# The first 40 microseconds of a fused graph kernel: second batch's xT loaded ahead of adj, its product with W0 made directly behind the first batch's, and the first loads issued from two queues in fewer requests

## The chip, the cores and the metric

The kernel runs on one core of one Trainium2 chip. The metric is the device time of one execution in microseconds. Before the change the median of three runs is 545.93 us (545.26 to 547.8).

## What is computed

There are 16 batches. Each has x (512 nodes by 256 features) and its own adjacency matrix adj (512 by 512). Two blocks follow each other, each with a residual and a layer norm:

```python
# block 0 (layer norm 1 behind it)
h = x @ W0 + b0
x = layernorm(x + (adj @ h) / adj.sum(-1))
# block 1 (layer norm 2 behind it)
y = relu(adj @ (x @ W1) + b1)
y = relu(adj @ (y @ W2) + b2)
x = layernorm(x + adj @ (y @ W3) + b3)
```

All is fp32. The kernel makes each fp32 product from three products of rounded parts: every operand is split into a "hi" part (rounded) and a "lo" part (what is left), and hi·hi, lo·hi and hi·lo are added up in PSUM.

## The kernel before

Nodes lie on the 128 partitions in T = 4 tiles, features in KF = 2 halves. A batch goes through eight products on TensorE (PE), named by their helper functions: `p0` (xT times W0, into h), `p1` (adj times h), `p2` (x1 times adj, into g), `p3` (W1 times g, into x2), `p4` (x2 times W2, into s2), `p5`, `p6` and `p7` (the third layer). `three_passes` issues the three matmuls of one product; they show as lines 180, 181 and 182. Behind each product ScalarE (ACT) rounds the result into a hi tile (`copy_hi`, line 486) and VectorE (DVE) subtracts it into a lo tile (`sub_hi`, line 676). GpSimd (POOL) makes the lo tiles of adj, adds b0 and b3, and in the first microseconds makes some lo tiles of x1 and the weights.

`norm1` is the first layer norm. On DVE it takes one tile a turn: a reciprocal of the row sum (it waits for `p1_done` of that tile), a scalar_tensor_tensor into v1 (it waits for POOL's `xb`, x plus b0), bn_stats and bn_aggr, and in the next turn, when ACT has made the square root (`std_1`), x1. A turn's x1 is what `p2` needs.

Every engine works through its own instructions in the order of the code, and waits on semaphores. In the steady part a loop runs `step(new)` for batch after batch, in which the products of two or three batches are interleaved by hand. Ahead of the loop stands a prologue, written out by hand for each engine, that brings batches `FIRST` and `second` to where the loop takes over; the loop's first matmul is that of `p5(FIRST)`. SP (the sync engine) issues all loads, in one queue. The second batch's xT goes into the buffer `y`, its x into `v` (`v2`), its adjT into `adj_rows`, since those aren't needed yet.

In the prologue `p1_first`, `p2_first` and `p0_first` are forms of the products that start as soon as the first operands are there. PE's prologue before:

```python
p0_first()
p1_first(range(0, T // 2)); p1_first(range(T // 2, T))
p0(second, None, None, bank_a)
p2_first(range(0, 1)); p1(second, range(0, 1))
p2_first(range(1, T)); p1(second, range(1, 2))
p3(FIRST); p1(second, range(2, 3))
p4(FIRST); p1(second, range(3, T))
```

and DVE's, of which the second half (from `norm1(FIRST, range(3, ...))` on) is the same in both kernels but for a split of W1:

```python
split_xT(second, 0); split_xT(second, 1)
norm1(FIRST, range(0, 3)); h(second, bank_a)
norm1(FIRST, range(3, T + 2)); norm1(second, range(0, 1))
g(FIRST, 0); g(FIRST, 1); norm1(second, range(1, 2))
x2(FIRST, 0); x2(FIRST, 1); norm1(second, range(2, 3))
s2(FIRST); norm1(second, range(3, T + 2))
```

Of the kernel before, what the change touches and what calls it, by code (L numbers as in the profile page):

```python
# [18 lines left out]

def build(nc, xT, x, adjT, adj, w0, w1, w2, w3, b0, b1, b2, b3, out):  # L20
    NB = x.shape[0]
# [7 lines left out]
    with ExitStack() as ctx:  # L29
# [12 lines left out]
        b0_all = sb("b0_all", [P, F], F32)
        b3_all = sb("b3_all", [P, F], F32)
        b1_col = sb("b1_col", [P, KF], F32)
        b2_col = sb("b2_col", [P, KF], F32)
# [53 lines left out]
        adj0_even_split = sem("adj0_even_split")  # L99
        x1_first_split = sem("x1_first_split")  # L100
# [106 lines left out]
        def _(sp):  # L207
# [17 lines left out]
            for half in range(2):  # L225
                tiles = half_of(half, T)
                sp.dma_start(adj1_raw[:, tiles, :], adjT[1, :, tiles, :]).then_inc(adj1_loaded[half], DMA)
            sp.dma_start(w_raw[:, 1, :, :], w1).then_inc(w_loaded[1], DMA)
            sp.dma_start(x1_raw[:, :, :], x[1]).then_inc(x1_loaded, DMA)
            sp.dma_start(b3_all[:, :], b3.partition_broadcast(P)).then_inc(b_loaded[3], DMA)  # L230
            sp.dma_start(w_raw[:, 2, :, :], w2).then_inc(w_loaded[2], DMA)
            sp.dma_start(b1_col[:, :], b1).then_inc(b_loaded[1], DMA)
            sp.dma_start(b2_col[:, :], b2).then_inc(b_loaded[2], DMA)
            sp.dma_start(w_raw[:, 3, :, :], w3).then_inc(w_loaded[3], DMA)

# [248 lines left out]
        def _(act):  # L484
# [115 lines left out]
            def step(new, last=False, ahead=True):  # L600
# [21 lines left out]
            split_adj(FIRST, 0)  # L622
            h(FIRST, tiles=range(0, 1))
            split_adj(FIRST, 1)
            h(FIRST, tiles=range(1, 3))
            split_adj(FIRST, 2)
            h(FIRST, tiles=range(3, T))
            split_adj(FIRST, 3)
# [8 lines left out]
            h(second, bank_a, range(0, 1))
            x1_split_hi(FIRST, 0)
            h(second, bank_a, range(1, T))
            std_1(FIRST, 2)  # L640
            x1_split_hi(FIRST, 1)
            split_w(1)
            std_1(FIRST, 3)
            x1_split_hi(FIRST, 2)
            x1_split_hi(FIRST, 3)
            norm1(second, None, range(0, 1))
# [215 lines left out]
        def _(pool):  # L862
# [55 lines left out]

            for k in range(0, T, 2):
                pool.wait_ge(adj_hi_ready, k + 1)  # L920
                pool.tensor_tensor(adj_lo[:, 0, k, :], adj_raw[:, k, :], adj_hi[:, 0, k, :].bitcast(F32),
                                   ALU.subtract).then_inc(adj0_even_split, 1)
            pool.wait_ge(b_loaded[0], DMA)
# [11 lines left out]
            pool.wait_ge(b_loaded[3], DMA)  # L935
            add_b3(FIRST, range(0, 2))
# [45 lines left out]
```

## Time and profile before

| | |
|---|---|
| median of three runs | 545.93 us |
| the profiled execution: its own time, its span | 545.0 us, 543.2 us |
| PE busy | 531.9 us, 98% of the span |
| DVE, ACT, POOL busy | 351.8, 311.0, 212.1 us |
| all idle time of PE that the waits list | 6.6 us, all of it in the first 38 us |
| granted TensorE clock, mean | 0.994 |
| DMA | 58.23 MB, mean 107 GB/s |

The span is what the profiler saw from the first to the last instruction. PE's busy share is near one from slice to slice; only the first two slices of 40 and the last one are lower. The prologue ends at 41.56 us, when the loop's first matmul starts.

### The profile page before, as it was taken

What the parts mean: (1) busy time and instruction counts of PE and PEld (TensorE: products, weight loads), DVE (VectorE), ACT (ScalarE), POOL (GpSimd) and SP (SyncE); (2) the same over time, 40 slices, a digit from 0 to 9 for tenths busy, and PEclk for the clock granted to TensorE, in tenths of its full rate; (3) what the DMA queues carried; (4) which work ended last, traced back from release to release, by engine and by line L of the source; (5) the groups of instructions that cost most, each with busy time, mean ns of one, the idle gap of its engine ahead of it and who ended that gap; (6) DMA issues with size and microseconds to landing.
All of it is one profiled execution on the core that took longest, in us unless ns stands there. A gap on an engine that the chain in (4) does not pass through costs nothing.

```text
span 543.2 us, 10642 instructions
## 1 busy us (share of the span) xinstructions
PE 531.9 (98%) x3637; PEld 490.4 (90%) x3637; DVE 351.8 (65%) x1058; ACT 311.0 (57%) x786; POOL 212.1 (39%) x228
## 2 busy tenths in 40 slices
PE   7899999999999999999999999999999999999996
PEld 6878999989899898999989899898998989899896
DVE  4774675757667485675757667475675757657546
ACT  4555655566555746655566554756655566564542
POOL 2866318072360904408062270814509063271100
PEclk9999999999999999999999999999999999999998
DMA  8630060602507043070612507033070511600002
GB/s 275 226 140 1 30 244 0 238 36 65 206 0 270 0 137 133 11 259 0 214 56 60 211 0 270 0 124 146 0 270 0 192 79 50 222 1 40 1 1 78
DMA packets 15286, 58.23 MB, mean 107 GB/s; under 512 B 1952, under 2 KB 2720, under 8 KB 13472
## 3 DMA queue, kind: packets, MB, share of 16 engines
q1 hardware_dynamic: 15264, 57.94, 29.5%
q8 instruction: 13, 0.21, 0.2%
q14 instruction: 9, 0.07, 0.0%
HBM read 49.55 MB, written 8.39 MB: 107 GB/s over the span
## 4 chain that ended last, share of the span: by engine, by line
PE 92%; DVE 4%; DMA 2%; ACT 1%; issue 1%; SPq 1%; DVEq 0%
PE bank_a L181 16%; PE bank_a L182 16%; PE bank_a L180 16%; PE bank_b L180 14%; PE bank_b L182 14%; PE bank_b L181 14%; DMA y<-in_xT 2%; PE bank_b L273 1%; PE bank_b L274 1%; DVE x L744 0%; DVE v L737 0%; DVE xT_lo L676 0%; DVE stats L748 0%; DVE x_lo L676 0%; DVE stats L787 0%
## 5 line engine op out<-in xcount | busy, mean ns | idle before, releaser
L900 POOL TENSOR_TENSOR adj_lo<-adj_raw,adj_hi 128x512 fp32r<-128x512 f32 x56 | 70.8, 1298 | 264.2 <-ACT adj_hi L486 264.2
L676 DVE TENSOR_TENSOR x_lo<-bank_a,x_hi 128x512 fp32r<-128x512 f32 x62 | 42.8, 691 | 67.7 <-ACT bank_a L576 67.7
L180 PE MATMUL bank_b<-h_hi,adj_hi 128*128 128x256 f32 (+1 forms) x256 | 71.7, 280 | 2.2 <-DVE h_lo L676 2.2
L551 ACT ACTIVATE std<-moments,eps_col 128x1 f32<-128x1 f32 x64 | 18.9, 295 | 92.4 <-DVE moments L757 92.4
L182 PE MATMUL bank_b<-h_hi,adj_lo 128*128 128x256 f32 (+1 forms) x256 | 71.5, 279 | 0.0
L181 PE MATMUL bank_b<-h_lo,adj_hi 128*128 128x256 f32 (+1 forms) x256 | 71.5, 279 | 0.0
L182 PE MATMUL bank_b<-s_hi,adj_lo 128*128 128x256 f32 x232 | 64.1, 276 | 0.0
L180 PE MATMUL bank_b<-s_hi,adj_hi 128*128 128x256 f32 x232 | 64.0, 276 | 0.0
L181 PE MATMUL bank_b<-s_lo,adj_hi 128*128 128x256 f32 x232 | 64.0, 276 | 0.0
L574 ACT ACTIVATE x_hi<-bank_a,b_col 128x512 fp32r<-128x512 f32 x62 | 42.4, 684 | 21.4 <-PE bank_a L182 20.2
L882 POOL TENSOR_TENSOR x1b<-x,b_all 128x256 f32<-128x256 f32 x64 | 46.0, 754 | 17.2 <-DVE x L744 17.2
L180 PEld LDWEIGHTS bank_b<-h_hi,adj_hi 128*128 128x128 f32 x256 | 48.9, 191 | 2.3 <-issue 2.3
L180 PE MATMUL bank_a<-adj_hi,s_hi 128*128 128x512 f32 x128 | 50.1, 391 | 0.0
L181 PE MATMUL bank_a<-adj_lo,s_hi 128*128 128x512 f32 x128 | 50.0, 390 | 0.0
L182 PE MATMUL bank_a<-adj_hi,s_lo 128*128 128x512 f32 x128 | 49.8, 389 | 0.0
L181 PEld LDWEIGHTS bank_b<-h_lo,adj_hi 128*128 128x128 f32 x256 | 48.8, 191 | 0.0
L182 PEld LDWEIGHTS bank_b<-h_hi,adj_lo 128*128 128x128 f32 x256 | 48.8, 191 | 0.0
L595 ACT ACTIVATE std<-moments,eps_col 128x1 f32<-128x1 f32 x64 | 18.9, 295 | 51.9 <-DVE moments L799 51.9
L676 DVE TENSOR_TENSOR g_lo<-bank_a,g_hi 128x512 fp32r<-128x512 f32 x30 | 20.7, 691 | 40.2 <-ACT g_hi L486 40.2
L180 PE MATMUL bank_a<-adj_hi,x_hi 128*128 128x512 f32 x120 | 46.7, 389 | 0.0
L181 PE MATMUL bank_a<-adj_lo,x_hi 128*128 128x512 f32 x120 | 46.7, 389 | 0.0
L182 PE MATMUL bank_a<-adj_hi,x_lo 128*128 128x512 f32 x120 | 46.7, 389 | 0.0
(145 smaller groups left out, 1653.8 us busy)
## 6 DMA issues: line engine op xcount, KB each, us to landing
adj_raw<-in_adjT SPq DMA_DIRECT2D x30, 512.0 KB, 5.4
adj_rows<-in_adj SPq DMA_DIRECT2D x14, 1024.0 KB, 9.4
x_raw<-in_x SPq DMA_DIRECT2D x15, 512.0 KB, 7.4
out_y<-y SPq DMA_DIRECT2D x15, 512.0 KB, 2.9
xT_raw<-in_xT SPq DMA_DIRECT2D x14, 512.0 KB, 6.5
w_raw<-in_w SPq DMA_DIRECT2D x4, 256.0 KB, 10.2
adj_rows<-in_adjT SPq DMA_DIRECT2D x2, 512.0 KB, 10.1
xT_raw<-in_xT SPq DMA_DIRECT2D x2, 256.0 KB, 3.6
```

The source lines that it names most:

```text
L180: pe.matmul(acc, st[0], mv[0], start=start, stop=False)
L181: pe.matmul(acc, st[0], mv[1], start=False, stop=False)
L182: return pe.matmul(acc, st[1], mv[0], start=False, stop=stop)
L273: pe.matmul(bank[j][:, 0:2 * F], hi, w_both[:, n, k, :, :], start=True, stop=False)
L274: mm = pe.matmul(bank[j][:, 0:F], lo, mv[0], start=False, stop=False)
L551: act.activation(std1[:, j:j + 1], moments1[:, j, 1:2], ACT.Sqrt, bias=eps_col[:, :]).then_inc(std1_ready, 1)
L574: act.activation(hi[:, f, :], bank[:, :], ACT.Relu, bias=bias[:, f:f + 1])
L595: act.activation(std2[:, j:j + 1], moments2[:, j, 1:2], ACT.Sqrt, bias=eps_col[:, :]).then_inc(std2_ready, 1)
L676: return dve.tensor_tensor(lo, full, hi.bitcast(F32), ALU.subtract)
L882: pool.tensor_tensor(x1b[:, slot(batch), j, :], x1[:, j, :], b3_all[:, :], ALU.add).then_inc(x1b_ready, 1)
L900: pool.tensor_tensor(adj_lo[:, s, k, :], raw[:, k, :], adj_hi[:, s, k, :].bitcast(F32), ALU.subtract).then_inc(adj_split, 1)
```

## The change

It has four parts, all in the prologue; the loop and the end are untouched.

1. Loads. SP issues xT of batch 0 in one request, adjT's low half, b0 with b3 in one, the second adjT's low half, x of the second batch, W1 to W3 in one, b1 with b2 in one. ACT issues W0 and the second batch's xT at its very start, and behind its table load adjT's high half, x of batch 0 and the second adjT's high half. The host lays W1 to W3, b0 with b3, and b1 with b2 side by side for this.
2. PE. `p0(second)` stands directly behind `p0_first`. `p1_first` goes tile by tile. `p2_first` is made in one piece; `p1(second)` tile 0 stands behind it, tiles 1 and 2 behind `p3`, tile 3 behind `p4`.
3. ACT and DVE split the second batch's xT ahead of the first batch's h tiles 1 to 3 and of adj. POOL makes the lo part of one adj tile of batch 0 and DVE of three (before two and two). DVE makes W1's lo part.
4. ACT's order behind that: a `std_1`, an `x1_split_hi` and a `split_adj(second)` alternate; `h(second)` comes behind `std_1(FIRST, 2)` and waits for all of `p1_first`.

```diff
@@ sync @@
-            sp.dma_start(w_raw[:, 0, :, :], w0).then_inc(w_loaded[0], DMA)
-            for half in range(2):
-                tiles = half_of(half, T)
-                sp.dma_start(xT_raw[:, tiles, :], xT[0, :, tiles, :]).then_inc(xT0_loaded[half], DMA)
...
-            sp.dma_start(x_raw[:, :, :], x[0]).then_inc(x_loaded, DMA)
-            sp.dma_start(b0_all[:, :], b0.partition_broadcast(P)).then_inc(b_loaded[0], DMA)
-            sp.dma_start(xT1_raw[:, :, :], xT[1]).then_inc(xT_loaded, DMA)
...
+            sp.dma_start(xT_raw[:, :, :], xT[0]).then_inc(xT_loaded, DMA)
+            low = half_of(0, T)
+            sp.dma_start(adj_raw[:, low, :], adjT[0, :, low, :]).then_inc(adj_loaded[0], DMA)
+            sp.dma_start(b03_all[:, :], b03.partition_broadcast(P)).then_inc(b03_loaded, DMA)
+            sp.dma_start(adj1_raw[:, low, :], adjT[1, :, low, :]).then_inc(adj1_loaded[0], DMA)
+            sp.dma_start(x1_raw[:, :, :], x[1]).then_inc(x1_loaded, DMA)
+            sp.dma_start(w_raw[:, 1:4, :, :], w123).then_inc(w123_loaded, DMA)
+            sp.dma_start(b12_col[:, 0:2 * KF], b12).then_inc(b12_loaded, DMA)
@@ tensor @@
             p0_first()
+            p0(second, None, None, bank_a)
             pe.wait_ge(ones_set, 2 * T)
-            p1_first(range(0, T // 2))
-            p1_first(range(T // 2, T))
-
-            p0(second, None, None, bank_a)
-            p2_first(range(0, 1))
+            for j in range(T):
+                p1_first(range(j, j + 1))
+            p2_first(range(0, T))
             p1(second, range(0, 1))
-            p2_first(range(1, T))
-            p1(second, range(1, 2))
-            pe.wait_ge(w_split, 1)
+            pe.wait_ge(w1_split, 1)
             p3(FIRST)
-            p1(second, range(2, 3))
-            pe.wait_ge(w_split, 3)
+            p1(second, range(1, 3))
+            pe.wait_ge(w_split, 2)
             p4(FIRST)
             p1(second, range(3, T))
@@ scalar @@
+            high = slice(T // 2, T)
+            act.dma_start(w_raw[:, 0, :, :], w0).then_inc(w0_loaded, DMA)
+            act.dma_start(xT1_raw[:, :, :], xT[1]).then_inc(xT1_loaded, DMA)
             act.wait_ge(eps_set, 1)
             act.activation(sqrt_eps[:, :], eps_col[:, :], ACT.Sqrt)
+            act.dma_start(adj_raw[:, high, :], adjT[0, :, high, :]).then_inc(adj_loaded[1], DMA)
+            act.dma_start(x_raw[:, :, :], x[0]).then_inc(x_loaded, DMA)
+            act.dma_start(adj1_raw[:, high, :], adjT[1, :, high, :]).then_inc(adj1_loaded[1], DMA)
...
+            act.wait_ge(p1_done, T)
+            h(second, bank_a)
+            x1_split_hi(FIRST, 2)
             split_adj(second, 3)
...
@@ vector @@
-            h(FIRST, tiles=range(0, 2))
-            split_adj0(1)
-            h(FIRST, tiles=range(2, T))
-            split_adj0(3)
+            h(FIRST, tiles=range(0, 1))
             split_xT(second, 0)
             split_xT(second, 1)
+            h(FIRST, tiles=range(1, T))
+            split_adj0(0)
+            split_adj0(2, counts=2)
+            split_adj0(3)
             norm1(FIRST, range(0, 3))
             h(second, bank_a)
             norm1(FIRST, range(3, T + 2))
+            split_w1()
             norm1(second, range(0, 1))
             g(FIRST, 0)
             g(FIRST, 1)
@@ gpsimd @@
-            split_adj(second, range(0, 3))
+            split_adj(second, range(0, 1))
             split_x1_first(0)
+            split_adj(second, range(1, 2))
+            split_x1_first(1)
+            split_adj(second, range(2, 3))
+            split_x1_first(2)
             split_adj(second, range(3, T))
-            split_x1_first(1)
             add_b0(second, range(0, 1))
-            split_x1_first(2)
-            split_w(1)
             add_b0(second, range(1, T))
```

The order of PE's products from `p2_first` to the loop, one row for each product, before (`bank_b` with `x1_hi` is `p2_first`, `bank_a` with `h_hi` is `p1(second)` and its number is the tile, `bank_b2<-g_hi` begins `p3`, `bank_b0<-w_both,x2_hi` begins `p4`):

```order
L180 MATMUL bank_b0<-adj_hi,x1_hi 128x512
...
L180 MATMUL bank_a0<-h_hi,adj_hi 128x258
...
L180 MATMUL bank_b0<-adj_hi,x1_hi 128x512
...
L180 MATMUL bank_a1<-h_hi,adj_hi 128x258
...
L180 MATMUL bank_b2<-g_hi,w_both 128x512
...
L180 MATMUL bank_a2<-h_hi,adj_hi 128x258
...
L180 MATMUL bank_b0<-w_both,x2_hi 128x256
...
L180 MATMUL bank_a3<-h_hi,adj_hi 128x258
```

The same stretch of PE in the changed kernel:

```order
L184 MATMUL bank_b0<-adj_hi,x1_hi 128x512
...
L184 MATMUL bank_a0<-h_hi,adj_hi 128x258
...
L184 MATMUL bank_b2<-g_hi,w_both 128x512
...
L184 MATMUL bank_a1<-h_hi,adj_hi 128x258
...
L184 MATMUL bank_a2<-h_hi,adj_hi 128x258
...
L184 MATMUL bank_b0<-w_both,x2_hi 128x256
...
L184 MATMUL bank_a3<-h_hi,adj_hi 128x258
```

Tile 0 of `p1(second)` moved from inside `p2_first` to behind it, and tile 1 from ahead of `p3` to behind it. DVE's instructions between them did not move: this is DVE in the changed kernel, from the reciprocal of the second batch's tile 0 (`inv_rows<-bank_a`) to the lo parts of g and the reciprocal of tile 1:

```order
L726 RECIPROCAL inv_rows<-bank_a 128x1
L736 SCALAR_TENSOR_TENSOR v<-bank_a,inv_rows,xb 128x256
L747 BN_STATS stats<-v 128x6
L756 BN_AGGR moments<-stats 128x2
L670 TENSOR_TENSOR g_lo<-bank_b,g_hi 128x512 x2
L726 RECIPROCAL inv_rows<-bank_a 128x1
```

So tile 0 of norm1(second) still stands ahead of g's lo parts on DVE, and tile 1 ahead of x2's. ACT around `h(second)` before, from the split of the last xT half to its fourth h tile (`h_hi<-bank_a` are the h tiles of the second batch):

```order
L486 ACTIVATE xT_hi<-y 128x512 x2
L486 ACTIVATE adj_hi<-adj_rows 128x512
L551 ACTIVATE std<-moments,eps_col 128x1
L486 ACTIVATE adj_hi<-adj_rows 128x512 x2
L551 ACTIVATE std<-moments,eps_col 128x1
L486 ACTIVATE adj_hi<-adj_rows 128x512
L486 ACTIVATE h_hi<-bank_a 128x256
L486 ACTIVATE x_hi<-x 128x256
L486 ACTIVATE h_hi<-bank_a 128x256 x3
```

And ACT in the changed kernel, from the first h tile of batch 0 to the same place:

```order
L474 ACTIVATE h_hi<-bank_b 128x256
L474 ACTIVATE xT_hi<-y 128x512 x2
L474 ACTIVATE h_hi<-bank_b 128x256 x3
L474 ACTIVATE adj_hi<-adj_raw 128x512 x4
L474 ACTIVATE adj_hi<-adj_rows 128x512
L542 ACTIVATE std<-moments,eps_col 128x1
...
L474 ACTIVATE adj_hi<-adj_rows 128x512
L542 ACTIVATE std<-moments,eps_col 128x1
L474 ACTIVATE h_hi<-bank_a 128x256 x4
```

The second batch's xT now comes ahead of all four adj tiles of the first, and the h tiles of the second batch come behind the third `std` instead of the second.

## Rows read from the trace of the kernel before

**Rows 1.** Windows: length, busy (instructions) of PE, PEld, DVE, ACT, POOL, PEclk, DMA share, GB/s

```profile
9.00:11.40 2.40, 0.42 (x3) 0.45 (x4) 1.37 (x4) 2.40 (x8) 1.38 (x2) 0.99 0.94 352
11.40:14.70 3.30, 3.30 (x18) 3.30 (x17) 2.44 (x5) 1.80 (x5) 3.30 (x4) 0.50 1.02 414
41.60:75.00 33.40, 33.40 (x231) 30.80 (x231) 21.02 (x64) 18.67 (x48) 13.22 (x14) 1.00 0.23 82
```

**Rows 2.** The chain that ended last, 0 to 45 us: start, length, what

```profile
1.80 0.42 SPq L217
...
2.74 0.43 SPq L221
3.21 0.43 SPq L222
...
4.16 9.18 DMA y<-in_xT
...
14.03 2.15 DVE xT_lo L676 x2
...
22.02 1.30 DVE h_lo L676 x4
...
30.75 1.30 DVE g_lo L676 x2
```

**Rows 3.** DMA issues of single loads: out, in, KB, us from issue to landing

```profile
xT_raw<-in_xT SPq DMA_DIRECT2D x1, 256.0 KB, 3.7
...
adj_raw<-in_adjT SPq DMA_DIRECT2D x1, 512.0 KB, 7.2
x_raw<-in_x SPq DMA_DIRECT2D x1, 512.0 KB, 8.0
```

**Rows 4.** Timeline of PE: start, length, line, what, and the idle time ahead

```profile
5.63 0.47 PE L309 MATMUL bank_b<-w_both,xT_hi 128*128 128x256 f32 x2 [0.58 <-ACT xT_hi L486]
...
8.43 0.39 PE L315 MATMUL bank_b<-w_both,xT_lo 128*128 128x256 f32 x2
10.98 0.36 PE L180 MATMUL bank_b<-h_hi,adj_hi 128*128 128x258 f32 x1 [2.16 <-DVE h_lo L676]
...
29.82 0.39 PE L182 MATMUL bank_b<-adj_hi,x_lo 128*128 128x512 f32 x1
...
32.19 0.47 PE L180 MATMUL bank_b<-g_hi,w_both 128*128 128x512 f32 x1 [0.54 <-DVE g_lo L676]
...
35.02 0.28 PE L180 MATMUL bank_a<-h_hi,adj_hi 128*128 128x258 f32 x1
...
36.32 0.28 PE L182 MATMUL bank_a<-h_hi,adj_lo 128*128 128x258 f32 x1
37.32 0.36 PE L180 MATMUL bank_b<-w_both,x_hi 128*128 128x256 f32 x1 [0.73 <-DVE x_lo L676]
...
41.56 0.40 PE L180 MATMUL bank_a<-adj_hi,s_hi 128*128 128x512 f32 x1
```

**Rows 5.** Timeline of DVE

```profile
12.11 1.06 DVE L676 TENSOR_TENSOR adj_lo<-adj_raw,adj_hi 128x512 fp32r<-128x512 f32 x1
...
16.10 0.15 DVE L727 RECIPROCAL inv_rows<-bank_b 128x1 f32<-128x1 f32 x1
...
28.42 0.15 DVE L727 RECIPROCAL inv_rows<-bank_a 128x1 f32<-128x1 f32 x1
...
29.73 0.18 DVE L757 BATCH_NORM_AGGREGATE moments<-stats 128x2 f32<-128x6 f32 x1
...
31.96 0.16 DVE L727 RECIPROCAL inv_rows<-bank_a 128x1 f32<-128x1 f32 x1
...
33.72 0.18 DVE L757 BATCH_NORM_AGGREGATE moments<-stats 128x2 f32<-128x6 f32 x1
```

**Rows 6.** Timeline of ACT and of POOL

```profile
19.70 0.62 ACT L486 ACTIVATE adj_hi<-adj_rows 128x512 fp32r<-128x512 f32 x1
...
12.58 4.20 POOL L876 TENSOR_TENSOR xb<-x_raw,b_all 128x256 f32<-128x256 f32 x4
```

More of the change, by code:

```diff
@@ L17, with build @@
 WARM = 18
-def build(nc, xT, x, adjT, adj, w0, w1, w2, w3, b0, b1, b2, b3, out):
+def build(nc, xT, x, adjT, adj, w0, w123, b03, b12, out):
     NB = x.shape[0]
@@ L41, in build @@
         w_raw = sb("w_raw", [P, 4, KF, F], F32)
[L42 to L45, printed above, removed]
+        b03_all = sb("b03_all", [P, 2 * F], F32)
+        b0_all, b3_all = b03_all[:, 0:F], b03_all[:, F:2 * F]
+        b12_col = sb("b12_col", [P, 16], F32)
+        b1_col, b2_col = b12_col[:, 0:KF], b12_col[:, KF:2 * KF]
         zeros = sb("zeros", [P, F], F32R)
@@ L89, in build @@
         bank_a = [ctx.enter_context(nc.psum_tensor(f"bank_a{j}", [P, 512], F32)) for j in range(T)]
-        w_loaded = [sem(f"w{n}_loaded") for n in range(4)]
-        b_loaded = [sem(f"b{n}_loaded") for n in range(4)]
-        xT0_loaded = [sem(f"xT0_half{n}_loaded") for n in range(2)]
+        w0_loaded = sem("w0_loaded")
+        w123_loaded = sem("w123_loaded")
+        b03_loaded = sem("b03_loaded")
+        b12_loaded = sem("b12_loaded")
+        xT1_loaded = sem("xT1_loaded")
         xT_loaded = sem("xT_loaded")
@@ L98, in build @@
         adj1_loaded = [sem(f"adj1_half{n}_loaded") for n in range(2)]
-        adj0_even_split = sem("adj0_even_split")
+        adj0_second_split = sem("adj0_second_split")
         x1_first_split = sem("x1_first_split")
@@ L109, in build @@
         w_hi_ready = sem("w_hi_ready")
+        w1_split = sem("w1_split")
         w_split = sem("w_split")
@@ L213, in _ @@
             sp.sem_inc(rows_ready, 2 * T)
-            sp.dma_start(w_raw[:, 0, :, :], w0).then_inc(w_loaded[0], DMA)
-            for half in range(2):
-                tiles = half_of(half, T)
-                sp.dma_start(xT_raw[:, tiles, :], xT[0, :, tiles, :]).then_inc(xT0_loaded[half], DMA)
-            for half in range(2):
-                tiles = half_of(half, T)
-                sp.dma_start(adj_raw[:, tiles, :], adjT[0, :, tiles, :]).then_inc(adj_loaded[half], DMA)
-            sp.dma_start(x_raw[:, :, :], x[0]).then_inc(x_loaded, DMA)
-            sp.dma_start(b0_all[:, :], b0.partition_broadcast(P)).then_inc(b_loaded[0], DMA)
-            sp.dma_start(xT1_raw[:, :, :], xT[1]).then_inc(xT_loaded, DMA)
[L225 to L228, printed above, removed]
-            sp.dma_start(x1_raw[:, :, :], x[1]).then_inc(x1_loaded, DMA)
[L230 to L234, printed above, removed]
+            sp.dma_start(xT_raw[:, :, :], xT[0]).then_inc(xT_loaded, DMA)
[3 more added lines that the diff above has]
+            sp.dma_start(adj1_raw[:, low, :], adjT[1, :, low, :]).then_inc(adj1_loaded[0], DMA)
+            sp.dma_start(x1_raw[:, :, :], x[1]).then_inc(x1_loaded, DMA)
+            sp.dma_start(w_raw[:, 1:4, :, :], w123).then_inc(w123_loaded, DMA)
+            sp.dma_start(b12_col[:, 0:2 * KF], b12).then_inc(b12_loaded, DMA)
             def load(i):
@@ L322, in p1_first @@
                     pe.wait_ge(h_split, max(k + 1, len(tiles)))
-                    if k % 2 == 0:
-                        pe.wait_ge(adj0_even_split, k // 2 + 1)
+                    if k == 1:
+                        pe.wait_ge(adj0_second_split, 1)
                     else:
@@ L488, in split_w @@
             def split_w(n):
-                act.wait_ge(w_loaded[n], DMA)
+                act.wait_ge(w123_loaded, DMA)
                 copy_hi(w_hi[:, n, :, :], w_raw[:, n, :, :]).then_inc(w_hi_ready, 1)
@@ L495, in split_xT @@
                 tiles = slice(half * T // 2, (half + 1) * T // 2)
-                if nxt is FIRST:
-                    act.wait_ge(xT0_loaded[half], DMA)
+                if nxt is second:
+                    act.wait_ge(xT1_loaded, DMA)
+                elif nxt is FIRST:
+                    act.wait_ge(xT_loaded, DMA)
                 else:
                     act.wait_ge(xT_loaded, at(nxt, DMA, 0))
+                if nxt is not FIRST:
                     act.wait_ge(p0_done, at(nxt, T, 0))
@@ L616, in step @@
                     norm1(nxt, before(new, -2) if ahead else None)
+            high = slice(T // 2, T)
+            act.dma_start(w_raw[:, 0, :, :], w0).then_inc(w0_loaded, DMA)
+            act.dma_start(xT1_raw[:, :, :], xT[1]).then_inc(xT1_loaded, DMA)
             act.wait_ge(eps_set, 1)
             act.activation(sqrt_eps[:, :], eps_col[:, :], ACT.Sqrt)
+            act.dma_start(adj_raw[:, high, :], adjT[0, :, high, :]).then_inc(adj_loaded[1], DMA)
+            act.dma_start(x_raw[:, :, :], x[0]).then_inc(x_loaded, DMA)
+            act.dma_start(adj1_raw[:, high, :], adjT[1, :, high, :]).then_inc(adj1_loaded[1], DMA)
             split_xT(FIRST, 0)
             split_xT(FIRST, 1)
-            split_adj(FIRST, 0)
             h(FIRST, tiles=range(0, 1))
[L624 to L628, printed above, removed]
             split_xT(second, 0)
             split_xT(second, 1)
+            h(FIRST, tiles=range(1, T))
+            for k in range(T):
+                split_adj(FIRST, k)
             split_adj(second, 0)
             std_1(FIRST, 0)
+            x1_split_hi(FIRST, 0)
             split_adj(second, 1)
+            std_1(FIRST, 1)
+            x1_split_hi(FIRST, 1)
             split_adj(second, 2)
-            std_1(FIRST, 1)
+            std_1(FIRST, 2)
+            act.wait_ge(p1_done, T)
+            h(second, bank_a)
+            x1_split_hi(FIRST, 2)
             split_adj(second, 3)
[L637 to L641, printed above, removed]
+            std_1(FIRST, 3)
+            x1_split_hi(FIRST, 3)
             split_w(1)
[L643 to L646, printed above, removed]
             g(FIRST, 0)
             g(FIRST, 1)
+            norm1(second, None, range(0, 1))
             split_w(2)
             split_w(3)
-            act.wait_ge(b_loaded[1], DMA)
-            act.wait_ge(b_loaded[2], DMA)
+            act.wait_ge(b12_loaded, DMA)
             x2(FIRST, 0)
@@ L682, in split_xT, with split_adj0, split_w1 @@
                 sub_hi(xT_lo[:, tiles, :], raw[:, tiles, :], xT_hi[:, tiles, :]).then_inc(xT_split, 1)
-            def split_adj0(k):
+            def split_adj0(k, counts=1):
                 dve.wait_ge(adj_hi_ready, k + 1)
-                sub_hi(adj_lo[:, 0, k, :], adj_raw[:, k, :], adj_hi[:, 0, k, :]).then_inc(adj_split, 2)
+                sub_hi(adj_lo[:, 0, k, :], adj_raw[:, k, :], adj_hi[:, 0, k, :]).then_inc(adj_split, counts)
+            def split_w1():
+                dve.wait_ge(w_hi_ready, 1)
+                sub_hi(w_lo[:, 1, :, :], w_raw[:, 1, :, :], w_hi[:, 1, :, :]).then_inc(w1_split, 1)
             def join(bank, half):
@@ L821, in _ @@
                 dve.memset(h_lo[:, j, F:F + ONES].bitcast(F32), 0.0).then_inc(ones_set, 1)
-            dve.wait_ge(w_loaded[0], DMA)
+            dve.wait_ge(w0_loaded, DMA)
             dve.tensor_copy(w_hi[:, 0, :, :], w_raw[:, 0, :, :]).then_inc(w0_hi_ready, 1)
@@ L828, in _ @@
             split_xT(FIRST, 1)
-            h(FIRST, tiles=range(0, 2))
-            split_adj0(1)
-            h(FIRST, tiles=range(2, T))
-            split_adj0(3)
+            h(FIRST, tiles=range(0, 1))
             split_xT(second, 0)
             split_xT(second, 1)
+            h(FIRST, tiles=range(1, T))
+            split_adj0(0)
+            split_adj0(2, counts=2)
+            split_adj0(3)
             norm1(FIRST, range(0, 3))
@@ L917, in step @@
                 add_b3(new)
[L919 to L923, printed above, removed]
+            pool.wait_ge(adj_hi_ready, 2)
+            pool.tensor_tensor(adj_lo[:, 0, 1, :], adj_raw[:, 1, :], adj_hi[:, 0, 1, :].bitcast(F32),
+                               ALU.subtract).then_inc(adj0_second_split, 1)
+            pool.wait_ge(b03_loaded, DMA)
             add_b0(FIRST)
             pool.wait_ge(adj_split, T)
-            split_adj(second, range(0, 3))
+            split_adj(second, range(0, 1))
             split_x1_first(0)
+            split_adj(second, range(1, 2))
+            split_x1_first(1)
+            split_adj(second, range(2, 3))
+            split_x1_first(2)
             split_adj(second, range(3, T))
-            split_x1_first(1)
             add_b0(second, range(0, 1))
-            split_x1_first(2)
-            split_w(1)
             add_b0(second, range(1, T))
-            pool.wait_ge(b_loaded[3], DMA)
             add_b3(FIRST, range(0, 2))
@@ L966 @@
     }
-    for n, name in enumerate(("L0_gnn_W", "L1_gnn_W1", "L1_gnn_W2", "L1_gnn_W3")):
-        arrays[f"w{n}"] = np.asarray(inputs[name]).reshape(KF, P, F).transpose(1, 0, 2)
-    arrays["b0"] = np.asarray(inputs["L0_gnn_b"])
-    arrays["b1"] = np.asarray(inputs["L1_gnn_b1"]).reshape(KF, P).T
-    arrays["b2"] = np.asarray(inputs["L1_gnn_b2"]).reshape(KF, P).T
-    arrays["b3"] = np.asarray(inputs["L1_gnn_b3"])
+    w = [np.asarray(inputs[name]).reshape(KF, P, F).transpose(1, 0, 2)
+         for name in ("L0_gnn_W", "L1_gnn_W1", "L1_gnn_W2", "L1_gnn_W3")]
+    arrays["w0"] = w[0]
+    arrays["w123"] = np.stack(w[1:], axis=1)
+    arrays["b03"] = np.concatenate([np.asarray(inputs["L0_gnn_b"]), np.asarray(inputs["L1_gnn_b3"])])
+    arrays["b12"] = np.concatenate([np.asarray(inputs["L1_gnn_b1"]).reshape(KF, P).T,
+                                    np.asarray(inputs["L1_gnn_b2"]).reshape(KF, P).T], axis=1)
     arrays = {f"in_{k}": np.ascontiguousarray(a) for k, a in arrays.items()}
```

## The prediction

> **What bounds the kernel now.** I read the windows first. In the loop PE is busy for all of 33.40 us in a stretch of 33.40, at the full granted clock [rows 1]. So nothing that only shortens another engine's work counts there, and since the loop's code is untouched, the change is worth what it moves the loop's first matmul, which starts at 41.56 [rows 4]. The rest of the program then follows at the same distance.
>
> Next, the chain that ended last, for the first 45 us. It does not start at adj but at the second batch's xT: its load is issued at 4.16 and takes 9.18 us, so it lands at 13.34; the two xT_lo on DVE keep that engine until 16.1; then comes norm1 of the first batch [rows 2, 5]. The timeline of PE shows what is lost meanwhile: PE idles 2.16 us ahead of `p1_first` (10.98) [rows 4], and from 11.40 to 14.70 the granted clock is 0.50, the lower of its two levels (1.2 GHz) [rows 1]. Eighteen matmuls took 3.30 us there, which at full clock would take half, so that stretch costs 1.65 us. These two, together 3.8 us, are what the change can reach for, and `p0(second)` placed in the gap is the way to it.
>
> I cut the prologue at five places, all read off the rows. S is the start of norm1(FIRST) on DVE, 16.10 [rows 5]. The last h_lo of the second batch ends at 22.02 + 1.30 = 23.32 [rows 2], 7.22 later. The last matmul of `p2_first` starts at 29.82, 6.50 later; `p3` at 32.19, 2.37 later; `p4` at 37.32, 5.13 later; the loop at 41.56, 4.24 later [rows 4]. Together 16.10 + 7.22 + 6.50 + 2.37 + 5.13 + 4.24 = 41.56.
>
> **Term 1, the start of norm1(FIRST).** Before, 768 KB (W0 and the first xT) were down at 1.80 + 3.7 = 5.5, 1792 KB (with adjT) at 2.74 + 7.2 = 9.9, and 2304 KB at 3.21 + 8.0 = 11.2 [rows 2, 3]. From 9 to 14.7 the 16 DMA engines were busy for 0.94 to 1.02 of the time, at 352 to 414 GB/s [rows 1]: they were full from one queue. I therefore take that a second queue brings no more bytes and that the two share in turns. Then W0 and xT land together at about 5.5, and the second xT and adjT's low half together after 1792 KB, at 9.9. `p0_first` took 5.63 to 8.82 [rows 4]; it now starts some 0.5 us later, because the first xT half no longer lands ahead and DVE gets W0 later, and it ends at 9.3 to 9.9. ACT can't overwrite xT_hi before that. So whether the second xT lands at 5.5 (alone and first) or at 9.9 hardly matters; only if it came with 2304 KB, at 11.2, would it cost another 1.3 us. From landing to the first xT_lo took 0.69 us (13.34 to 14.03) [rows 2], and the lo itself takes 0.7 to 1.1 (half of 2.15, with POOL working beside it). PE idles until about 11.4, then makes `p0(second)`: 24 matmuls, which with twelve of `p1` take 4.24 us ahead of the loop, where twelve of `p1` alone take 35.02 to 36.44, 1.42; so 2.82, until 14.2 [rows 4]. Behind xT_hi ACT has three h and four adj copies, at up to 0.62 each [rows 6]; the third lo tile of adj that DVE makes (0.7 to 1.06 each [rows 5]) comes at 15.3 to 15.9, and the first tile of `p1_first` is done 0.6 later, at about 16.3.
>
> The other leg is x: it needs 3584 KB ahead of it and with it, which is 1.84 MB more than at 9.9, or 4.4 to 5.2 us at the rates above, so it lands at 14.3 to 15.1; the first xb on POOL follows in 1.05 (a quarter of 4.20) [rows 6]. That gives 15.4 to 16.2. So S is about 16.3, not earlier than the 16.10 of before: what the early xT gives DVE, the late adj and PE's new order take. Bounds: 15.0 if both queues together run ahead of the old byte count, 17.8 if the gap of PE (9.9 to 11.4) is again followed by a stretch at 0.50 as in rows 1, which would add 1.65. The 2.16 gap did that; this one is some 1.5, and I leave it out.
>
> The Trainium skill, DMA: Bandwidth & Descriptors, section "Issuing engines are not separate DMA queues", says that DMAs of all issuing engines run on the same 16 DMA engines and that a second issuer saves only sequencer time. By that the landings stay as just worked out; if two queues did carry twice the bytes, x would be down before 12 and S would be PE's leg alone, near 15.
>
> **Term 2, to the end of h_lo.** In the order of ACT the h tiles of the second batch now stand behind the third std and a split of adj. DVE's turns of norm1 are as before, so ACT's copies come on top: between none and two at 0.62 [rows 6]. I take 0.9: 8.1 instead of 7.22.
>
> **Term 3, to the last matmul of p2_first.** The chain is norm1's last tile, and stays: 6.5. PE has less to do inside it, since `p1(second)` tile 0 is no longer between the pieces, but that doesn't move the chain's end.
>
> **Term 4, to p3.** Here a wait is added. DVE's order has norm1(second) tile 0 ahead of g's two lo tiles, and it waits for `p1(second)` tile 0, which before was long done and now runs behind `p2_first`. From the last `p2_first` matmul: 0.23 for it; 1.58 for the twelve matmuls and their drain (35.02 to 36.60) [rows 4]; norm1 of one first tile, 28.42 to 29.91, 1.49 [rows 5]; two g_lo and PE's start, 30.75 to 32.19, 1.44 [rows 2, 4]. Sum 4.74 instead of 2.37. PE idles some 3.1 us of it.
>
> **Term 5, to p4.** The same again one step on: norm1(second) tile 1 stands ahead of x2's lo tiles on DVE and waits for `p1(second)` tile 1, which now runs behind `p3`. `p3` 2.83 (32.19 to 35.02), tile 1 of `p1` 1.58 [rows 4], norm1 of a later tile 31.96 to 33.90, 1.94 [rows 5], of which I take 1.7 since POOL has gone quiet by then; two lo tiles and PE's start 1.44 as above. Sum 7.55 instead of 5.13. Term 6, `p4` and tile 3, stays 4.24: tile 2 is already made.
>
> **Term 7, the clock.** The idle 3.1 us ahead of `p3` is longer than the 2.16 us that went before the half clock of rows 1. I count one such stretch behind it, 1.4 (bounds 0 and twice 1.65, since PE also waits some 2.5 us inside `p2_first`, where part is hidden by the chain).
>
> **The sum.** 16.3 + 8.1 + 6.5 + 4.74 + 7.55 + 4.24 = 47.4, and 1.4 for the clock, 48.8: the loop starts 7.3 us later. On the profiled execution, 545.0, that is 552.3; the median of before lies 0.9 above it, so on the medians' scale 553.2. I give 552.7. The fewer requests themselves I cost at nothing: SP's issue times stand in the chain only ahead of the second xT [rows 2], and that part is in term 1. All work left is the same, so the loop hides nothing of a late start.
>
> **The rivals.** (a) The forecast: both new waits on DVE, one half-clock stretch, 550.5 to 555; chance 0.58. (b) The same waits, but no half clock, and loads that run ahead, S 15.0: 15.0 + 8.1 + 6.5 + 4.7 + 7.4 + 4.24 = 45.9, so 4.4 later, 549 to 550.5; chance 0.20. For it: the gaps are broken by short work. (c) Two or three half-clock stretches, or the second xT with 2304 KB: another 1.7 to 3, so 555 to 558; chance 0.11. (d) The waits are there but small, because S comes at 13.5 to 14 by faster loads and an early adj split: within 0.5% (2.7 us, about what a measurement here can tell from no change); chance 0.07. Against it: PE's own 24 matmuls behind 9.9, and 12 more. (e) Faster: the chain begins at the second xT, and that lands 3.4 us sooner (9.9 for 13.34). If DVE did not have to wait for `p1(second)`, all behind it would move up, the idle 2.16 and the half clock would be gone, and the end would be at 542 to 543. The point that decides is whether the two waits of terms 4 and 5, together 4.8 us, can be hidden; in order of code nothing can pass them. S would have to be below 16.10 - 0.9 - 2.4 - 2.4 = 10.4 to win in spite of them. Chance 0.04. That the loads don't come sooner at all is in (c).
>
> Slower takes (a), (b) and (c), 0.89; no change 0.07; faster 0.04. The range holds (a), (b) without its lowest part and half of (c): 548.7 to 556.
>
> **What would show it.** In the changed profile: PE idle about 3 us ahead of `p3`, released by DVE's g_lo, with the second batch's tile 0 of norm1 just ahead of it; PE idle 1.5 to 2 us ahead of `p4`, released by x2_lo; norm1(FIRST) starting near 16.3; `p0(second)` starting near 11.4; the loop's first matmul near 48 and 33.4 us of full PE behind it; the clock at 0.50 somewhere between 33 and 39. I am wrong if g_lo isn't held up by norm1(second), if adj's halves land before 9, or if the loop itself changes length.

## The result and the profile after

The changed kernel takes 555.42 us (median of four, 553.48 to 555.72) against 546.77 us of four runs of the kernel before beside it. The ratio is 1.0167, with a 95% interval of 1.0148 to 1.0187: it is slower, by 1.5 to 1.9%. The profiled execution took 555.47 us with a span of 553.7. One execution of the experiments, of e1, took 648.57 us at a mean granted clock of 0.835, and counts in no median or ratio below.

First the timeline of PE in the changed kernel, the rows that answer to [rows 4] (start, length, line, what, idle time ahead and its releaser). The line numbers are those of the changed kernel: 184 to 186 are the three passes, 474 is `copy_hi`, 670 `sub_hi`.

```profile
6.67 0.47 PE L300 MATMUL bank_b<-w_both,xT_hi 128*128 128x256 f32 x2 [1.44 <-ACT xT_hi L474]
...
11.37 0.38 PE L184 MATMUL bank_a<-w_both,xT_hi 128*128 128x256 f32 x1 [1.51 <-DVE xT_lo L670]
...
16.52 0.36 PE L184 MATMUL bank_b<-h_hi,adj_hi 128*128 128x258 f32 x1 [0.56 <-DVE adj_lo L670]
...
27.75 0.50 PE L184 MATMUL bank_b<-adj_hi,x_hi 128*128 128x512 f32 x1 [2.20 <-POOL x_lo L893]
...
33.00 0.63 PE L186 MATMUL bank_b<-adj_hi,x_lo 128*128 128x512 f32 x1
...
38.85 0.62 PE L184 MATMUL bank_b<-g_hi,w_both 128*128 128x512 f32 x1 [2.86 <-DVE g_lo L670]
...
47.90 0.36 PE L184 MATMUL bank_b<-w_both,x_hi 128*128 128x256 f32 x1 [1.64 <-DVE x_lo L670]
...
52.24 0.39 PE L184 MATMUL bank_a<-adj_hi,s_hi 128*128 128x512 f32 x1
```

The loop starts at 52.24 instead of 41.56, 10.7 us later, and the span grew by 10.5: behind the loop's start the two kernels agree within 0.2. The gap of 2.16 us in front of `p1_first` [rows 4] is gone; in its place PE waits 1.51 us ahead of `p0(second)` and 0.56 inside `p1_first`. The waits ahead of `p3` and `p4` grew from 0.54 and 0.73 [rows 4] to 2.86 and 1.64. Inside `p2_first` PE waits 1.00, 2.20 (the row at 27.75) and 0.87 us; before, the profile lists 0.85 and 0.52 there.

DVE in the changed kernel shows what holds g_lo and x2_lo up (answers to [rows 5], with the h_lo and g_lo of [rows 2]):

```profile
12.83 3.54 DVE L670 TENSOR_TENSOR adj_lo<-adj_raw,adj_hi 128x512 fp32r<-128x512 f32 x3
17.15 0.17 DVE L726 RECIPROCAL inv_rows<-bank_b 128x1 f32<-128x1 f32 x1 [0.78 <-PE bank_b L186]
...
24.03 1.42 DVE L670 TENSOR_TENSOR h_lo<-bank_a,h_hi 128x256 fp32r<-128x256 f32 x4 [0.83 <-ACT h_hi L474]
...
36.03 0.17 DVE L726 RECIPROCAL inv_rows<-bank_a 128x1 f32<-128x1 f32 x1 [4.25 <-PE bank_a L186]
...
37.45 1.26 DVE L670 TENSOR_TENSOR g_lo<-bank_b,g_hi 128x512 fp32r<-128x512 f32 x2
44.88 0.17 DVE L726 RECIPROCAL inv_rows<-bank_a 128x1 f32<-128x1 f32 x1 [6.18 <-PE bank_a L186]
...
46.50 1.26 DVE L670 TENSOR_TENSOR x_lo<-bank_b,x_hi 128x512 fp32r<-128x512 f32 x2
```

DVE stands still for 4.25 us until `p1(second)` tile 0 is done, works through that tile's norm1, and only then makes g_lo, though ACT had g_hi ready at 34.3. The same stands one product on: 6.18 us of waiting for tile 1, and x2_lo behind it.

The granted clock, by windows of the changed kernel (columns as in [rows 1]):

```profile
24.00:28.80 4.80, 2.60 (x11) 1.81 (x12) 4.02 (x12) 1.94 (x7) 2.92 (x3) 1.00 0.28 101
28.80:35.60 6.80, 5.93 (x20) 4.62 (x19) 2.02 (x3) 2.13 (x4) 4.96 (x7) 0.50 0.76 251
35.60:39.00 3.40, 0.54 (x4) 0.36 (x4) 2.43 (x6) 1.33 (x3) 0.54 (x1) 1.00 0.68 270
39.00:42.40 3.40, 3.40 (x9) 2.62 (x10) 0.00 (x0) 0.69 (x2) 3.34 (x4) 0.50 0.01 2
52.20:85.60 33.40, 33.40 (x231) 30.84 (x230) 20.62 (x63) 18.62 (x48) 13.25 (x14) 1.00 0.24 80
```

There are two stretches at 0.50, together 10.2 us, against one of 3.3 us before. Ahead of the first PE was busy for 2.60 us of 4.80, ahead of the second for 0.54 us of 3.40. The last row is the loop, the same 231 matmuls in 33.40 us as in [rows 1].

The loads of the changed kernel, issue to landing (as [rows 3]), with the issue of the second xT from ACT's timeline:

```profile
1.16 0.45 ACTq L611 DMA_DIRECT2D y<-in_xT  x1
...
xT_raw<-in_xT SPq DMA_DIRECT2D x1, 512.0 KB, 5.0
y<-in_xT ACTq DMA_DIRECT2D x1, 512.0 KB, 6.5
...
x_raw<-in_x ACTq DMA_DIRECT2D x1, 512.0 KB, 10.4
```

The second xT lands at 1.16 + 6.5 = 7.7 instead of 13.3. It can't be used at once: ACT rounds it into xT_hi, which `p0_first` reads until 9.86, and ACT's copy starts at 9.96.

### The profile page after: what moved, and what is told of

Read it like the earlier page. It is cut to its first block, busy times and chain, and to the rows that moved or that the text cites. A ratio compares the mean times of both kernels' runs of the same rounds, so it can differ in the third digit from the quotient of the medians.

```text
span 553.7 us, 10644 instructions
## 1 busy us (share of the span) xinstructions
PE 535.8 (97%) x3637; PEld 492.4 (89%) x3637; DVE 353.4 (64%) x1060; ACT 311.1 (56%) x786; POOL 209.5 (38%) x226
## 4 chain that ended last, share of the span: by engine, by line
PE 92%; DVE 4%; ACT 1%; DMA 1%; issue 1%; DVEq 0%; SPq 0%; ACTq 0%
PE bank_a L185 16%; PE bank_a L184 16%; PE bank_a L186 16%; PE bank_b L184 14%; PE bank_b L185 14%; PE bank_b L186 14%; PE bank_b L264 1%; DMA xT_raw<-in_xT 1%; DVE adj_lo L670 1%; PE bank_b L265 1%; DVE x L743 1%; DVE v L736 0%; DVE h_lo L670 0%; DVE stats L786 0%; DVE x_lo L670 0%
```

## The experiments

All profiles are of one execution each; ratios are to the kernel before, run beside them (37 executions of it beside e1 to e7). "Loop at" is the start of the loop's first matmul.

| kernel | median us | ratio to before (95%) | span | norm1(FIRST) | loop at |
|---|---|---|---|---|---|
| before | 545.5, 545.6 | | 543.2 | 16.10 | 41.56 |
| changed | 555.42 | 1.0167 (1.0148 to 1.0187) | 553.7 | 17.15 | 52.24 |
| e1: before, p1(second) late on PE | 553.06 | 1.0134 (1.0111 to 1.0157) | 550.3 | 16.01 | 48.66 |
| e2: changed, g_lo first on DVE | 552.59 | 1.0107 (1.0079 to 1.0135) | 550.8 | 18.34 | 49.30 |
| e3: changed, g_lo and x2_lo first | 549.24 | 1.0051 (1.0032 to 1.0070) | 547.6 | 16.58 | 46.15 |
| e4: changed, filling ahead of p3 | 551.95 | 1.0107 (1.0087 to 1.0127) | 553.1 | 18.04 | 51.65 |
| e5: changed, filling in p2_first too | 551.16 | 1.0094 (1.0080 to 1.0108) | 550.9 | 18.14 | 49.47 |
| e6: before with the new loads | 544.14 | 0.9972 (0.9962 to 0.9983) | 542.4 | 15.38 | 40.88 |
| e6 again | 544.17 | 0.9966 (0.9954 to 0.9979) | 542.4 | 15.36 | 40.96 |
| e7: e6 and the new front | 547.00 | 1.0020 (1.0005 to 1.0035) | 544.6 | 16.65 | 43.15 |

Wherever the loop starts, what follows to the end of the span is 501.4 to 501.6 us in every one of them (for the changed kernel 553.7 - 52.24, for e6 542.4 - 40.88).

**e1, one part alone: the order of p1(second) on PE.** In the kernel before:

```diff
-            p2_first(range(0, 1))
-            p1(second, range(0, 1))
-            p2_first(range(1, T))
-            p1(second, range(1, 2))
+            p2_first(range(0, T))
+            p1(second, range(0, 1))
             pe.wait_ge(w_split, 1)
             p3(FIRST)
-            p1(second, range(2, 3))
+            p1(second, range(1, 3))
```

> The kernel before with one part of the change alone: PE makes p2_first in one piece, p1(second) tile 0 behind it, tiles 1 and 2 behind p3, tile 3 behind p4. Loads, ACT, DVE and POOL as before. Theory A (the new order of p1(second) makes DVE wait in front of g_lo and x2_lo, and the idle time brings stretches at half clock): 5 to 8 us slower than before, PE idle 2.5 to 3.5 us ahead of p3 and 1 to 2 us ahead of p4, one stretch at 0.50 behind the first of these. Rival B (the loss comes from the front: W0, adj and x late through the second queue, and p0(second) ahead of p1_first): within 1 us of before, since none of that is in this kernel.

PE of this kernel at `p3` and `p4`:

```profile
35.48 0.77 PE L180 MATMUL bank_b<-g_hi,w_both 128*128 128x512 f32 x1 [3.82 <-DVE g_lo L674]
...
44.44 0.36 PE L180 MATMUL bank_b<-w_both,x_hi 128*128 128x256 f32 x1 [1.63 <-DVE x_lo L674]
```

and its windows, of which the second is the stretch behind that gap:

```profile
28.00:35.00 7.00, 3.66 (x22) 2.84 (x20) 2.74 (x7) 1.77 (x5) 3.89 (x6) 1.00 0.59 228
35.30:38.60 3.30, 3.12 (x7) 2.48 (x8) 0.03 (x1) 0.34 (x2) 3.30 (x4) 0.50 0.10 42
```

The loop starts 7.1 us later than before, with norm1(FIRST) where it was (16.01). Rival B is out as the main cause: without any of the new loads or the new front, 1.34 of the 1.67% are there. The gap ahead of `p3` came out 3.82, longer than the 2.5 to 3.5 expected, because in this kernel ACT too waits for norm1(second) ahead of g_hi: its square root for that tile starts at 33.23 and g_hi at 33.44, where the changed kernel's g_hi starts at 32.38, ahead of the square root.

**e2 and e3, the two waits taken away.** In the changed kernel DVE makes g_lo (e2), and x2_lo as well (e3), ahead of the norm1 tile that waits. e3:

```diff
-            norm1(second, range(0, 1))
             g(FIRST, 0)
             g(FIRST, 1)
-            norm1(second, range(1, 2))
+            norm1(second, range(0, 1))
             x2(FIRST, 0)
             x2(FIRST, 1)
+            norm1(second, range(1, 2))
```

> The changed kernel, but DVE makes the two g_lo tiles ahead of norm1(second) tile 0; nothing else. Theory A: the idle 2.9 us ahead of p3 goes, and with it most of the stretch at half clock behind it (39.0 to 42.5): 3.5 to 5 us faster than the changed kernel, so 3.5 to 5.5 us slower than before. Rival B: no faster than the changed kernel by more than 1 us, since what is late then is late from the front on.

> As the last one, and DVE makes the two x2_lo tiles ahead of norm1(second) tile 1 as well. Theory A: the idle 1.6 us ahead of p4 goes too; 1 to 1.6 us faster than the last kernel, unless the two turns of norm1 now stand in front of s2_lo and hold up the loop's first matmul (then less than 1 us). Rival B: as the last kernel.

PE of e3 lists no wait ahead of `p3`, and ahead of `p4` a small one for another engine, POOL's lo part of W2:

```profile
30.12 0.80 PE L184 MATMUL bank_b<-adj_hi,x_hi 128*128 128x512 f32 x1 [0.91 <-DVE x_lo L670]
41.88 0.39 PE L184 MATMUL bank_b<-w_both,x_hi 128*128 128x256 f32 x1 [0.86 <-POOL w_both L888]
```

By the ratios e2 gives back 0.6 of the 1.67% and e3 another 0.56, so about two thirds of the loss lay behind two swaps on DVE. By the profiles, counted from norm1(FIRST) so that the front drops out, the way to the loop is 25.5 us before, 35.1 in the changed kernel, 31.0 in e2 and 29.6 in e3. The 4.1 us that e3 has over the kernel before are 1.1 up to the end of h_lo (the forecast's term 2), 1.5 from there to `p3`, with a stretch at 0.50 still there from 28.2 to 35.0, and 1.5 from `p3` to `p4`. What of them ACT's and POOL's new order costs was not run by itself. e2's last gap grew to 2.58 us ahead of `p4`, since PE now comes there earlier while x2_lo still waits; that is what e3 takes away. e2's expectation was missed: it is 2.8 us faster than the changed kernel by the medians and 3.3 by the ratios, not 3.5 to 5, since a stretch at 0.50 stood at 44.5 to 48 instead; counted from norm1(FIRST) it is 4.1. e3's was exceeded: 3 us, not 1 to 1.6.

**e4 and e5, the clock as a term of its own.** The waits stay, but PE makes matmuls of zeros while it waits; nothing of the output changes. e5:

```diff
-            p2_first(range(0, T))
+            p2_first(range(0, 2))
+            pe.wait_ge(h_split, 2 * T)
+            fill(bank_a[T - 1], 16)
+            p2_first(range(2, 3))
+            fill(bank_a[T - 1], 6)
+            p2_first(range(3, T))
             p1(second, range(0, 1))
+            fill(bank_b[T - 1], 22)
```

> The changed kernel, with 22 matmuls of zeros (128 by 256, into a bank that p3 overwrites) put on PE between p1(second) tile 0 and p3, so that PE is not idle while it waits for g_lo; the wait itself stays, and the output too. Theory A with the clock as a term of its own: p3 no longer starts at half clock; the stretch 39.0 to 42.5 goes, 1.5 to 2 us faster than the changed kernel. Rival C (the clock term is not bound to the idle time): no change, or slower by the filling.

> As the last one, and fillings of 16 and 6 such matmuls inside p2_first, ahead of its third and fourth k, behind a wait for the second batch's h_lo. Theory A with the clock as a term: the stretch at half clock from 28.8 to 35.6 goes as well; p2_first's last part and p1(second) tile 0 take 2.8 us instead of 5, so 3 to 4.5 us faster than the changed kernel in all, and still 4 to 5.5 us slower than before by the two waits. Rival C: no faster than the last kernel.

e5, windows from `p2_first` to the loop, and PE at its `p3`, `p4` and the loop:

```profile
26.00:30.00 4.00, 3.92 (x24) 3.13 (x23) 3.25 (x10) 1.12 (x3) 2.12 (x4) 1.00 0.13 50
30.00:37.60 7.60, 6.84 (x48) 6.11 (x46) 4.27 (x9) 3.36 (x7) 5.13 (x7) 1.00 0.82 274
37.60:49.40 11.80, 10.10 (x72) 9.45 (x73) 6.00 (x19) 6.03 (x15) 3.61 (x4) 1.00 0.12 49
```

```profile
37.67 0.47 PE L184 MATMUL bank_b<-g_hi,w_both 128*128 128x512 f32 x1 [0.23 <-DVE g_lo L680]
...
45.14 0.36 PE L184 MATMUL bank_b<-w_both,x_hi 128*128 128x256 f32 x1 [1.63 <-DVE x_lo L680]
...
49.47 0.40 PE L184 MATMUL bank_a<-adj_hi,s_hi 128*128 128x512 f32 x1
```

With PE kept at work there is no stretch at 0.50 behind norm1(FIRST), and from its start (18.14) to the loop it takes 31.3 us instead of 35.1, with both waits in place. So 3.8 us of the loss in the changed kernel's profile are the lower clock. The ratios agree: e5 is 0.73% better than the changed kernel, 4.0 us, within its expectation of 3 to 4.5. In e4 the stretch behind `p3` is gone (its `p3` to `p4` takes 7.5 us, not 9.05) and the one inside `p2_first` stays. Rival C falls. e4 was expected 1.5 to 2 us faster than the changed kernel; its profiled execution has 1.5 from norm1(FIRST) to the loop, but its median is better by 0.60%, 3.3 us. Three of its six executions took 550.89 to 550.95 us at a mean granted clock of 0.999 or 1.000, as fast as e5, so the stretch inside `p2_first` was not there in them, though the filling stands behind it; all four executions of the changed kernel are at 0.988 to 0.993. Why is not shown. e4 is therefore no clean price of the stretch behind `p3`, and the 0.13% between e4 and e5 lies within the intervals.

**e6, the loads alone.** The kernel before, with SP's and ACT's requests of the change and no other order moved:

```diff
+            act.dma_start(w_raw[:, 0, :, :], w0).then_inc(w0_loaded, DMA)
+            act.dma_start(xT1_raw[:, :, :], xT[1]).then_inc(xT1_loaded, DMA)
...
+            act.dma_start(adj_raw[:, high, :], adjT[0, :, high, :]).then_inc(adj_loaded[1], DMA)
+            act.dma_start(x_raw[:, :, :], x[0]).then_inc(x_loaded, DMA)
+            act.dma_start(adj1_raw[:, high, :], adjT[1, :, high, :]).then_inc(adj1_loaded[1], DMA)
             split_xT(FIRST, 0)
```

> The kernel before with the first part of the change alone: loads in two queues, fewer requests, the second xT second in ACT's queue; every engine's order of work as before. Theory A: p0_first starts about 1 us later (W0 and the first xT land together), the second xT lands near 7.7 instead of 13.3, so DVE's xT_lo no longer hold up norm1(FIRST), which starts 0 to 1 us earlier: within 1 us of before, either way. Rival B: the loads are a good part of the loss: 2 us or more slower than before, with norm1(FIRST) at 17 us.

> The kernel before with the loads of the change alone, once more beside the one with the front: again 0.1 to 0.4% faster than before (theory A: norm1(FIRST) at 15.4 instead of 16.1, and no stretch at half clock); 0 if the first result was the luck of the clock.

DVE and PE of e6:

```profile
13.07 2.38 DVE L674 TENSOR_TENSOR xT_lo<-y,xT_hi 128x512 fp32r<-128x512 f32 x2
15.38 0.15 DVE L725 RECIPROCAL inv_rows<-bank_b 128x1 f32<-128x1 f32 x1
```

```profile
11.40:14.70 3.30, 3.16 (x27) 2.99 (x26) 3.30 (x6) 2.24 (x5) 3.30 (x3) 1.00 1.03 422
```

```profile
10.94 0.36 PE L183 MATMUL bank_b<-h_hi,adj_hi 128*128 128x258 f32 x1 [1.58 <-DVE h_lo L674]
...
40.88 0.40 PE L183 MATMUL bank_a<-adj_hi,s_hi 128*128 128x512 f32 x1
```

DVE goes on to the xT_lo at once instead of waiting 0.86 us for their load and ACT's copies, norm1(FIRST) starts 0.7 us earlier, and the loop follows 0.7 earlier. PE idles 1.58 us instead of 2.16 ahead of `p1_first`, and the stretch at 0.50 that stood there in [rows 1] is at 1.00: 27 matmuls in 3.30 us instead of 18. It is 0.3% faster than before in both tries (1.4 us by the medians, a little more than the 1 us expected), and the fastest kernel of the study, so rival B falls for the loads. Its 18 runs lie within 543.97 and 544.40, while 37 runs of the kernel before lie within 544.53 and 547.95; the early half-clock stretch is the likely source of that spread, which was not shown run by run.

**e7, the loads and the front.** e6 with `p0(second)` directly behind `p0_first`, the front orders of ACT, DVE and POOL, and the wait for `p1_first` ahead of h(second):

```diff
             p0_first()
+            p0(second, None, None, bank_a)
             pe.wait_ge(ones_set, 2 * T)
             p1_first(range(0, T // 2))
             p1_first(range(T // 2, T))
-
-            p0(second, None, None, bank_a)
```

> The kernel with the new loads alone (546.6 to 543 on its span), and now the front of the change too: p0(second) directly behind p0_first, the second xT split ahead of h tiles 1 to 3 and of adj, adj_lo three on DVE and one on POOL, a wait for all of p1_first ahead of h(second). Behind that PE, ACT, DVE and POOL as before. If the front itself helps: 1 us or more faster than the kernel with the loads alone. If what it gives DVE early it takes with the late adj, as the prediction's first term has it: norm1(FIRST) starts at 16.5 to 17.2 instead of 15.4, and it is 1 to 2.5 us slower than the loads alone.

(The first sentence of that expectation gives e6's span wrongly; it is 542.4.) DVE and PE of e7:

```profile
12.33 3.54 DVE L671 TENSOR_TENSOR adj_lo<-adj_raw,adj_hi 128x512 fp32r<-128x512 f32 x3
16.65 0.17 DVE L722 RECIPROCAL inv_rows<-bank_b 128x1 f32<-128x1 f32 x1 [0.78 <-PE bank_b L185]
```

```profile
23.42 0.50 PE L183 MATMUL bank_b<-adj_hi,x_hi 128*128 128x512 f32 x1 [3.61 <-POOL x_lo L888]
```

norm1(FIRST) starts at 16.65, 1.3 us later than in e6, because DVE's adj_lo come last; the loop starts 2.3 us later. The other 1.0 us lies behind norm1(FIRST): `p0(second)` used to fill the place between `p1_first` and `p2_first`, and with it gone PE waits 3.61 us there (1.36 ahead of `p2_first` in e6), followed by a stretch at 0.50 from 24.0 to 27.3; how much of the 1.0 is the lower clock was not tested. The ratio is 0.5% above e6's, 2.8 us, a little more than the 1 to 2.5 expected. So the front costs, and not by adj_lo alone.

By single profiles the loop's start goes from 41.56 by -0.7 (loads), +2.3 (front) and +9.1 (the order of `p2_first`, `p1(second)` and what ACT and POOL do around it) to 52.24.

## Why the prediction was right, and by how much it was off

The forecast was 552.7 us, 7.3 over the kernel before on either of the two scales it named; measured were 555.42, 8.65 over the kernel before beside it and, by the profiles, 10.7 at the loop's start (52.24, where the forecast had 48.8). The way and the mechanism were right: both waits on DVE are there where the prediction put them, and e1 to e3 show that they carry about two thirds of the loss. The size was not that of the favoured case (a), which ended at 555: with its two stretches at half clock the result is rival (c), which had a chance of 0.11. That the time still lies in the stated range is partly owed to half of (c) having been taken in. The band of 555 to 558 given for (c) does not follow from its own addition either: 1.7 to 3 us over 552.7 are 554.4 to 555.7. Here are the terms against the rows of the changed kernel, and against e5, which has the same order with the clock at 1.00 behind norm1(FIRST):

| step | predicted | changed | e5 |
|---|---|---|---|
| start of norm1(FIRST) | 16.3 | 17.15 | 18.14 |
| to the end of h_lo | 8.1 | 8.30 | 8.30 |
| to p3 (terms 3 and 4) | 11.24 | 13.40 | 11.23 |
| to p4 (term 5) | 7.55 | 9.05 | 7.47 |
| to the loop (term 6) | 4.24 | 4.34 | 4.33 |
| clock (term 7) | 1.4 | in the rows above | 0 |

**Terms 2 to 6** hold within 0.2 us in e5, where the clock is full. **Term 7, the clock**, was mis-sized: one stretch, 1.4 us, where the profile has two, worth 3.8 us (35.1 less 31.3, both from norm1(FIRST) to the loop). Its upper bound, twice 1.65, was too low as well, because I took each stretch at the 3.3 us of rows 1 and the first one here lasts 6.8. The idle time inside `p2_first` was under-sized too: the forecast had 2.5 us, the profile 4.1 (1.00, 2.20 and 0.87). Only the half clock of the third `p2_first` piece was hidden, since PE waits for x_lo behind it; that of the last piece and of tile 0 of `p1(second)` lies on the chain and makes the 2.2 us between 13.40 and 11.23. The second stretch, behind the wait ahead of `p3`, makes the 1.6 between 9.05 and 7.47, near the 1.4 that was forecast for it.

**Term 1** was 0.85 us short. Its loads came earlier than I had them (the second xT at 7.7, x at 2.13 + 10.4 = 12.5 instead of 14.3 to 15.1), and they did not matter, as the prediction said for xT and did not see for x. What came late was the third adj_lo: three of them took 3.54 us on DVE, 1.18 on average, where the forecast had 0.7 to 1.06, with POOL at work on its own adj_lo and xb in the same stretch (that POOL is the cause was not tested). `p0_first` started at 6.67 and ended at 9.86, at the late edge of 9.3 to 9.9, and `p0(second)` started at 11.37 as forecast.

**The Trainium skill's rule** (DMA: Bandwidth & Descriptors, "Issuing engines are not separate DMA queues"), that the loads of all issuing engines run on the same 16 DMA engines, agrees with the trace on bytes: in the changed kernel the engines were busy for 0.95 of the stretch from 5.0 to 9.9 at 354 GB/s, no more than the 352 to 414 of one queue. The loads still landed earlier than the forecast had them. Their order of issue is different, and from 4.5 to 6.0 the changed kernel moved 369 GB/s where the kernel before moved 117; which of the two did it was not tested, and the rule does not speak of it.

**The rivals.** (b) had the same waits without the half clock, and an S of 15.0. The first half of it is what e5 gives by filling the gaps; the S did not come, and the fastest execution of the changed kernel, 553.48, still has a mean granted clock of 0.993. (d), an S of 13.5 to 14, falls with 17.15. (e), faster, had the right chain: xT was late, and e6 shows that it is worth 0.3% as soon as nothing else is moved. But its condition alone, DVE not waiting for `p1(second)`, is e3, and that took 549.24, not 542 to 543.

What stays open is why the half-clock stretches fall in different places. e2's profile, with the same `p2_first` and the same wait of 2.20 us in it, has none there and one at 44.5 to 48.

## What to carry to other kernels

When a product is moved on one engine, look up its consumer on every other engine: an instruction that never waited because its input was old becomes a gate for all that is queued behind it, and here two such gates (2.86 and 1.64 us of idle PE) cost more than the gap of 2.16 that was filled. Read idle time of TensorE twice, once for itself and once for the lower clock behind it, which cost 3.8 us here. Look at the place that a moved product leaves, too: in e7 it became a gap of 3.61 us. Try the loads of a change by themselves first: here they were the only part that paid.

## What the hardware showed beyond that

In the profiles of e2, e4, e5 and the second one of e6 the 24 matmuls of `p0_first` ran 0.213 us apart for their first 3.3 to 4.5 us, nearly twice the usual 0.114, while the granted-clock column shows 1.00 there. These are the first rows of `p0_first` in e5 (each holds two matmuls), and the window over all 24:

```profile
6.01 0.77 PE L300 MATMUL bank_b<-w_both,xT_hi 128*128 128x256 f32 x2 [0.60 <-ACT xT_hi L484]
6.58 0.63 PE L303 MATMUL bank_b<-w_both,xT_hi 128*128 128x256 f32 x2
7.00 0.63 PE L306 MATMUL bank_b<-w_both,xT_lo 128*128 128x256 f32 x2
```

```profile
6.00:11.00 5.00, 4.83 (x24) 4.63 (x24) 1.62 (x3) 0.83 (x3) 0.00 (x0) 1.00 0.99 363
```

The warm-up matmuls ran at the same distance of 0.213 in every kernel, but for the last few in some (18 in 3.80 to 4.21 us), also at 1.00 in the column. A distance of 0.213 for 256 columns is that of the stretches at 0.50 (258 columns, 0.215 apart, from 33.42 on in the changed kernel). So the column can't be trusted ahead of its first change; the distance between matmuls can. In e2, e4 and e5 the start of norm1(FIRST) is 0.9 to 1.2 us later than in the changed kernel's own profile, and `p0(second)`, which waits for `p0_first`, is later by as much (12.25 to 12.56 instead of 11.37).
